# Another written order for the last attention phase of a 1-core kernel, with 34 more constant products on TensorE

## The chip, the cores and the metric

The kernel runs as one program on one core of one Trainium2 chip. The metric is the device time of one execution in microseconds (us). The kernel before took 2472.5 us (median of 3 executions, 2460.71 to 2488.86). All times from the trace are counted from the start of the profiled execution's span.

## The reference, cut to what matters

Two layers act on x, 8 sequences of 512 tokens of 128 features. Layer 0 is an attention with 16 heads of 8 features and a mixture of 16 experts; layer 1 is a gated cumulative mixer and a spiking feed-forward part. The change lies where layer 0's attention ends and its routing begins:

```
logits = S * scale + (G[..., :, None] - G[..., None, :])
P = softmax(where(tri, logits, -1e30));  o = P @ v;  x = x + ga * (o @ Wo)
h = layernorm(x) * (1 + cb) + sb
logits = -sum((h - keys)**2) + h @ rw.T + rb      # 16 experts per token
topv, topi = top_k(logits, 4);  w = softmax(topv)
x = x + gb * sum_k w_k * expert_{topi_k}(h)
```

The kernel sorts the tokens by expert first: for each token it finds the four experts and a row number (a slot) for each of them in a buffer in HBM, sends the token's row there four times, and later runs the experts over that buffer in pages of 128 rows.

## The kernel before, in words

Attention handles one sequence ("batch") at a time, in a **front half** (projections, the recurrence inside chunks of 16 tokens) and a **back half** (scores, softmax, values, output projection). A loop runs the back half of batch b beside the front half of batch b+1. After it there is one more phase, the **last attention phase**: the back half of batch 7 beside the **routing** of batches 0 to 6. The routing of batch 7 comes in the next block, with the experts; then comes layer 1.

In that phase each engine runs one instruction stream, woven of two by a string (`ORDER_END`, one entry per engine: 'pe' TensorE, 've' VectorE, 'act' ScalarE, 'po' GpSimd). A letter takes the next step of a stream: `b` of the back half, `r` of the routing, and `w`, on TensorE alone, one constant product (line 192): the 128x128 identity times itself, in float32, into PSUM bank 3, which nobody reads and for which nothing waits. Each profiled product is two instructions. The steps wait on semaphores for their data. The string decides only what stands ahead of what in an engine's own queue. The strings of before hold 175 `w`.

Back half, the steps in the order of TensorE's queue:
- **Stage A**, the chain of rotations: 7 times four products each of L1109 and L1116 and two of L1123, with copies by ScalarE (L555, L559) and VectorE (L828).
- **Stage B**, the row maxima: 40 jobs in 10 sets of four (m0 to m39). A job opens with L1156; its PSUM bank must have been read by the reduction (L833, VectorE) of the job four before. After the fourth opening come the set's score products (L1166 or L1160), and then the four reductions. Set 0 is m0 to m3.
- **Stage C**: a product of the maxima (L1173), its subtraction from the in-chunk scores on VectorE ("pdx", L853), their transposes ("pdT", L1179), exponentials, and 16 spreading products (rep0 to rep15, L1194), each multiplied on VectorE (L873) and added up half by VectorE (L884), half by GpSimd (oi0 to oi7: L439 and L446). VectorE's product 2i waits for oi(i-2); a rep waits for the product three before it; the stage after waits for all of them.
- **Stage D**, scores, exponentials and values: 14 groups of up to three jobs. S[k] are the group's score products (L1210, L1219, L1222), E[k] the one ScalarE exponential of it (L606), and v the value products (L1234). S[k+1] waits for E[k], since both use the same banks. v4 also waits until VectorE has copied the first block of results away ("raw0", L867).
- **Tail**: sums, transposes, output projection, x (to L939).

Routing of batch b: statistics and normalization (VectorE L1488, L1494, L1500, ScalarE L1442, L1447); transposes xT (L1622); ScalarE L1453, L1457; transposes back (bk, L1629); the **logit step** (four times L1640, L1641 and L1642: 12 products of 16 columns); top-4 on VectorE (L1507 to L1525, "chosen"); the count products (cnt, L1649 and L1650); slots on VectorE up to L1591; transposes and a product for the experts' bias (trn L1657, bia L1663) with VectorE's L1604 and L1610 on x. Then GpSimd sends the batch's rows: 16 indirect DMAs (L1436), 112 in the phase. GpSimd's queue also holds the masked copies "qsm" (L434), which wait for all 40 maxima, and oi0 to oi7.

The phase ends when every engine has done its part; the block of the experts then starts on all of them.

Of the kernel before, what the change touches and what calls it, by code (L numbers as in the profile page):

```python
# [120 lines left out]
def load_small(nc, dram, w, label):  # L121

    loaded = nc.alloc_semaphore(label + "_small")
    with nc.Block() as block:

        @block.sync
        def _(sp):
# [17 lines left out]
ORDER_FIRST = ('fffffffffffffffffffffffwfwffwwwwfwfwffwwwwfwfwffwwwwfwfwffwwwwfwfwffwwwwfwfwfwwfwwfwfwffwwwwfwfwffww'  # L145
           'wwfwfwffwwwwfwfwffwwwffffwwwffffwwfffwwwwwwwfwwwwwwwwwwwwfwwwwwwwwwwwwfwwwwwwwwwf')
ORDER_END = {
    'pe': ('brwwwwbbbbrbbbrrbbrbbbrwbrbbbbbbbwbbbbbbrbrbbbbbrbwwwbbwwwwrbbbbbbrwwbwwbwwbrwbbwwwbwwbwwbwwbbwwwwww'
           'bwwbwwbwwbbwwwrbbwwbwrbrbbbbbbwwbwwbwwbwwbbwbwwbwwbwwwwrbbwbwwbwwrwwwwrbwbbwwwwwwwwwwwwwwbwwwwwrbbww'
           'brrbwwwwwwwwwwwrwwwwwwrwwwwrwwbbwwwwwbbbbbbbbbwwbbwbbwbwrbbbrrbbbbbbwwwwrwbbbbbbbrwwbbbbrwwwbbbbbbbb'  # L150
           'bbwwwwbbbrbbbwrrbbbbbbbbwrbbbbbrbbwwbbbrbbbbwwbbbbbbbwwwwbbbbrbbbbbwrrbbbbbwwwrbbbbrbbbwwbbrrbbbbbbb'
           'bbbwwwbbbbbwwwwwwwwwwbwwwwb'),
    've': ('rrrrbrbbbrrrrrrrrrrrrrrrbbbrrrrrrrbbrrrrbbbrrrrrrrrrrrrrrrbbbbrrrrrbbbbrrrrbbbbrrbbbbbbbbrrbbbbrbbbb'
           'rrrrrrbbrrrrrbbrrrrrrrrrrrbrbbbbbbbbbbrrrrrrrrrrrrrrrbbbbrrrrrrrrrbbbbrbbbbbbbbbrbbbbbbbbbbbrrrrrrrr'
           'rrrrrrrrrrrrrbrrrrbrbrrrrrrrrrrrrrrrrrrrrrrrrrbrrrrrrrrrrrrrrrrrrrrrrrrrbbbbbbbbbbb'),
    'act': ('brrbrrbrrbbbrbbbbrrbbrrrbbbbbbbrbbbrrrrrbrrrrrrrrrrbbbrrrrrrbbrbbrrbrrrbrbrbbrrbrrrbrbrrbbb'),
    'po': ('bbbbbbbrrrrrrrrrrrrrrrrrrrrrrrrrrrrrrrrrrrrrrrrrrbrrrrrrrrrbbrbbbrbbrbrrrrrrrrrrrrrrrrrrrrrrrrrrrrrr'
           'rrrrrrrrrrrrrrrrrrrrrrrrrrrrr'),
}

# [2478 lines left out]
```

## Time and profile before

| | |
|---|---|
| median of 3 executions | 2472.5 us |
| profiled execution: its own time | 2484.16 us |
| profiled execution: span | 2482.4 us |
| mean granted TensorE clock | 0.888 of full |
| TensorE busy over the span | 84% |
| VectorE, ScalarE, GpSimd busy | 65%, 35%, 39% |
| last attention phase | 1461 to 1694 us |

The page gives the busy time of each engine; the last attention phase is about 9% of the span, so stretches of the trace are what is to be read. In a table of stretches each engine has its busy time and, in brackets, its number of instructions; then come the granted clock of TensorE (1.00 is 2.4 GHz, 0.50 is 1.2 GHz), the share of the DMA engines, and GB/s. In a timeline a row has start, duration, engine (PE is TensorE, DVE VectorE, ACT ScalarE, POOL GpSimd), line and operation, what is written and read, and the number of instructions merged into it; a bracket holds the engine's idle time before the row and what ended it. A busy TensorE is one with a product in flight.

### The profile page before, as it was taken

What the parts mean: (1) busy time and instruction counts of PE and PEld (TensorE: products, weight loads), DVE (VectorE), ACT (ScalarE), POOL (GpSimd) and SP (SyncE); (2) the same over time, 40 slices, a digit from 0 to 9 for tenths busy, and PEclk for the clock granted to TensorE, in tenths of its full rate; (3) what the DMA queues carried; (4) which work ended last, traced back from release to release, by engine and by line L of the source; (5) the groups of instructions that cost most, each with busy time, mean ns of one, the idle gap of its engine ahead of it and who ended that gap; (6) DMA issues with size and microseconds to landing.
All of it is one profiled execution on the core that took longest, in us unless ns stands there. A gap on an engine that the chain in (4) does not pass through costs nothing. (4 is left out here: it accounts for less than half of the span.)

```text
span 2482.4 us, 44309 instructions
## 1 busy us (share of the span) xinstructions
PE 2089.1 (84%) x16530; PEld 1388.0 (56%) x16530; DVE 1607.4 (65%) x3446; ACT 861.3 (35%) x1690; POOL 972.2 (39%) x999
## 2 busy tenths in 40 slices
PE   3888988987988988988988989997899982678885
PEld 2563653553663563563564567766899981334443
DVE  5968568568568568568558555733533334789986
ACT  2031331331331331232232222231366643477682
POOL 1514323314323314313313315753555558875221
PEclk7898998998998998898898888877999996799997
DMA  3102002002002002003003001115222221110000
GB/s 101 35 7 81 2 8 79 2 8 80 2 8 79 2 7 80 1 3 85 1 3 85 1 14 35 34 37 192 63 71 71 72 78 40 40 32 26 5 9 13
DMA packets 136618, 98.83 MB, mean 40 GB/s; under 512 B 14754, under 2 KB 127587, under 8 KB 136291
## 3 DMA queue, kind: packets, MB, share of 16 engines
q1 hardware_dynamic: 128226, 79.21, 10.9%
q0 software_dynamic: 8192, 16.79, 2.3%
q8 instruction: 146, 2.39, 0.4%
q14 instruction: 54, 0.43, 0.1%
HBM read 36.25 MB, written 55.57 MB: 37 GB/s over the span
## 5 line engine op out<-in xcount | busy, mean ns | idle before, releaser
L606 ACT ACTIVATE a_prep<-ps 128x1536 f32<-128x1536 f32 (+1 forms) x112 | 155.7, 1391 | 390.2 <-PE ps L1219 240.5
L413 POOL TENSOR_TENSOR a_K<-a_K,a_yU 128x480 f32<-128x480 f32 (+14 forms) x120 | 83.9, 699 | 423.6 <-DVE a_yU L782 423.6
L833 DVE TENSOR_REDUCE a_mpart<-ps 128x4 f32<-128x512 f32 x320 | 198.4, 680 | 62.2 <-PE ps L1160 58.1
L419 POOL TENSOR_TENSOR a_X<-a_X,a_txy 128x480 f32<-128x480 f32 (+14 forms) x240 | 177.8, 755 | 119.1 <-DVE a_txy L787 118.4
L1759 ACT ACTIVATE b_hid<-ps,b_stage 128x128 f32<-128x128 f32 x576 | 164.8, 369 | 138.3 <-PE ps L1863 138.3
L1743 POOL COPY b_stage<-b_w 128x1028 f32 x144 | 150.6, 1046 | 127.3 <-PE ps L1872 127.3
L1038 PE MATMUL ps<-a_txy,cst 128*128 128x480 f32 (+14 forms) x480 | 174.8, 472 | 7.8 <-DVE a_txy L769 7.8
L2003 POOL DMA_INDIRECT c_got<-rows_y,packed x128 | 151.4, 1183 | 38.3 <-issue 35.5
L787 DVE TENSOR_TENSOR a_txy<-a_wf,ps 128x480 f32<-128x480 f32 (+14 forms) x240 | 97.9, 417 | 88.2 <-PE ps L1038 85.7
L1863 PE MATMUL ps<-b_hTp,b_stage 128*128 128x128 f32 x1152 | 153.6, 277 | 0.0
L1872 PE MATMUL ps<-b_stage,b_hid 128*128 128x128 f32 x1152 | 152.3, 275 | 0.3 <-ACT b_hid L1759 0.3
L1436 POOL DMA_INDIRECT rows_h<-a_tS,r_slot x112 | 110.2, 984 | 101.6 <-issue 52.0
L769 DVE TENSOR_TENSOR a_txy<-a_bw,a_X 128x480 f32<-128x480 f32 (+14 forms) x240 | 142.4, 616 | 10.3 <-POOL a_X L419 10.3
L1863 PEld LDWEIGHTS ps<-b_hTp,b_stage 128*128 128x128 f32 x1152 | 141.5, 194 | 0.0
L1872 PEld LDWEIGHTS ps<-b_stage,b_hid 128*128 128x128 f32 x1152 | 140.2, 192 | 0.5 <-ACT b_hid L1759 0.5
L192 PE MATMUL ps<-cst 128*128 128x128 f32 x792 | 125.8, 307 | 14.4 <-PEq L209 14.4
L192 PEld LDWEIGHTS ps<-cst 128*128 128x128 f32 x792 | 112.0, 214 | 32.9 <-issue 28.9
L1156 PE MATMUL ps<-a_aux_g,a_g_hotb 24*128 24x512 bf16 (+1 forms) x320 | 104.2, 429 | 28.0 <-DVE a_mpart L833 26.6
L800 DVE TENSOR_TENSOR a_mats<-ps,cst 128x512 f32<-128x512 f32 x112 | 71.1, 683 | 75.8 <-PE ps L1067 75.8
L1835 DVE COPY b_hTp<-ps 128x128 f32<-128x128 f32 x144 | 41.9, 291 | 119.5 <-PE ps L1863 103.2
L1038 PEld LDWEIGHTS ps<-a_txy,cst 128*128 128x128 f32 x480 | 83.6, 215 | 63.6 <-DVE a_txy L769 34.4
L1032 PE MATMUL ps<-a_tU,cst 128*128 128x480 f32 (+14 forms) x240 | 93.1, 473 | 21.4 <-DVE a_tU L763 20.5
(469 smaller groups left out, 4658.7 us busy)
## 6 DMA issues: line engine op xcount, KB each, us to landing
rows_h<-a_blank SPq DMA_DIRECT2D x66, 512.0 KB, 6.5
b_hrow<-rows_h SPq DMA_DIRECT2D x144, 64.0 KB, 1.8
rows_y<-b_orow SPq DMA_DIRECT2D x144, 64.0 KB, 1.5
b_w<-in_wexp SPq DMA_DIRECT2D x16, 514.0 KB, 11.0
c_got<-rows_y,packed POOLq DMA_INDIRECT x128, 2.6
out<-xs SPq DMA_DIRECT2D x8, 256.0 KB, 2.3
cst<-in_const SPq DMA_DIRECT2D x1, 1865.5 KB, 14.7
rows_h<-a_tS,r_slot POOLq DMA_INDIRECT x112
```

What stands on the lines that cost most here:

```text
L192: nc.tensor.matmul(out, square, square, start=True, stop=True, skip_group_check=True)
L419: nc.gpsimd.tensor_tensor(x, x, yX[:, a, 0:n].rearrange("p (c s) -> p c s", c=NC), ALU.subtract).then_inc(e_uX.sem, 1)
L606: nc.scalar.activation(Pt[:, at:at + width, :], ps[:, 4:4 + width, :], ACT.Exp).then_inc(e_exp.sem, width)
L769: nc.vector.tensor_tensor(by_chunk(tX[:, a, 0:n]), chunks(bw[:, :])[:, :, left], chunks(X2[:, a, :])[:, :, right], ALU.mult).then_inc(e_tX ...
L833: nc.vector.tensor_reduce(mpart[:, i, j, 4 * g:4 * g + 4], ps[:, 4 + n % 4, :].rearrange("p (r j) -> p r j", r=4), AX.X, ALU.max).then_inc ...
L1038: mm(ps[:, 1 + a, 0:n], con("block8"), tX[:, a, 0:n], start=True, stop=True).then_inc(e_pX.sem, 1)
L1436: nc.gpsimd.indirect_dma_start(hrows, bass.IndirectOffsetOnAxis(R.slot[:, n, k:k + 1], 0), R.htok[:, b % 2, t, :], None).then_inc(R.e_sent ...
L1743: nc.gpsimd.tensor_copy(stage[:, p % 3, :], we[:, bass.ds(e, 1), :]).then_inc(e_stage.sem, 1)
L1759: last = nc.scalar.activation(hid[:, p % 2, f, :], ps[:, p % 2, 128 * f:128 * f + 128], ACT.Gelu, bias=stage[:, p % 3, AT_B1 + f:AT_B1 + f ...
L1863: last = mm(ps[:, q % 2, 128 * f:128 * f + 128], stage[:, q % 3, 128 * f:128 * f + 128], hTp[:, q % 2, :], start=True, stop=True, skip_gro ...
L1872: last = mm(ps[:, 4 + r % 2, 0:D], hid[:, r % 2, f, :], stage[:, r % 3, F + D * f:F + D * f + D], start=f == 0, stop=f == NF - 1, skip_gro ...
L2003: nc.gpsimd.indirect_dma_start(got[:, b % 2, k, t, :], None, yrows, bass.IndirectOffsetOnAxis(R.packed[:, n, k:k + 1], 0))\
```

## The change

Only the four strings of `ORDER_END` change. The numbers of `b` and of `r` stay the same on every engine (208 and 44 on TensorE, 98 and 185 on VectorE, 41 and 50 on ScalarE, 16 and 113 on GpSimd); `w` goes from 175 to 209. By stage of TensorE's queue the products are: up to m0 13, now 15; m0 to m39 82, now 87; stage C 33, now 42; from the first score group to cnt6 28, now 46; after that 19 and 19. What moves most:
- TensorE, stage B: logit step 2 goes from ahead of m20 to behind m24; xT2 from ahead of m16 to behind it; cnt2 from ahead of m31 to behind m33; trn2 and bia2 from behind m33 and ahead of m34 to behind m35; six products ahead of m12 become three.
- VectorE, stage B: chosen2 to eq2 (11 routing operations) go from ahead of max28 and max30 to, in the main, behind max31.
- VectorE, stage C: pdx goes behind the rest of routing 3 (L1575 to L1598). TensorE has 14 products instead of 2 ahead of pdT.
- TensorE, stage C: xT4 goes from behind rep12 to behind rep6, bk4 and logit step 4 from behind rep15 to behind rep8; six products then stand ahead of S[0].
- GpSimd: four sends of batch 3, not three, ahead of oi0; three, not one, between oi4 and oi5.
- Stage D: eight products, not four, ahead of cnt4; VectorE does part4, in4 and the statistics of batch 5 (L1604 to L1494) ahead of raw0, and 14 products, not 3, stand between v3 and v4; ScalarE does hT5 and hsq5 (L1453, L1457) ahead of E[4]; logit step 6 goes from the middle of S[10] to behind it; cnt6 from ahead of S[11] to behind it and v31.

```
--- before.py
+++ after.py
@@ -145,16 +145,16 @@
 ORDER_FIRST = ('fffffffffffffffffffffffwfwffwwwwfwfwffwwwwfwfwffwwwwfwfwffwwwwfwfwffwwwwfwfwfwwfwwfwfwffwwwwfwfwffww'
            'wwfwfwffwwwwfwfwffwwwffffwwwffffwwfffwwwwwwwfwwwwwwwwwwwwfwwwwwwwwwwwwfwwwwwwwwwf')
 ORDER_END = {
-    'pe': ('brwwwwbbbbrbbbrrbbrbbbrwbrbbbbbbbwbbbbbbrbrbbbbbrbwwwbbwwwwrbbbbbbrwwbwwbwwbrwbbwwwbwwbwwbwwbbwwwwww'
-           'bwwbwwbwwbbwwwrbbwwbwrbrbbbbbbwwbwwbwwbwwbbwbwwbwwbwwwwrbbwbwwbwwrwwwwrbwbbwwwwwwwwwwwwwwbwwwwwrbbww'
-           'brrbwwwwwwwwwwwrwwwwwwrwwwwrwwbbwwwwwbbbbbbbbbwwbbwbbwbwrbbbrrbbbbbbwwwwrwbbbbbbbrwwbbbbrwwwbbbbbbbb'
-           'bbwwwwbbbrbbbwrrbbbbbbbbwrbbbbbrbbwwbbbrbbbbwwbbbbbbbwwwwbbbbrbbbbbwrrbbbbbwwwrbbbbrbbbwwbbrrbbbbbbb'
-           'bbbwwwbbbbbwwwwwwwwwwbwwwwb'),
-    've': ('rrrrbrbbbrrrrrrrrrrrrrrrbbbrrrrrrrbbrrrrbbbrrrrrrrrrrrrrrrbbbbrrrrrbbbbrrrrbbbbrrbbbbbbbbrrbbbbrbbbb'
-           'rrrrrrbbrrrrrbbrrrrrrrrrrrbrbbbbbbbbbbrrrrrrrrrrrrrrrbbbbrrrrrrrrrbbbbrbbbbbbbbbrbbbbbbbbbbbrrrrrrrr'
-           'rrrrrrrrrrrrrbrrrrbrbrrrrrrrrrrrrrrrrrrrrrrrrrbrrrrrrrrrrrrrrrrrrrrrrrrrbbbbbbbbbbb'),
-    'act': ('brrbrrbrrbbbrbbbbrrbbrrrbbbbbbbrbbbrrrrrbrrrrrrrrrrbbbrrrrrrbbrbbrrbrrrbrbrbbrrbrrrbrbrrbbb'),
-    'po': ('bbbbbbbrrrrrrrrrrrrrrrrrrrrrrrrrrrrrrrrrrrrrrrrrrbrrrrrrrrrbbrbbbrbbrbrrrrrrrrrrrrrrrrrrrrrrrrrrrrrr'
+    'pe': ('brwwwwwbbbbbrbbrrbbbbbbrbbbbrbrbbbbbbbbbbbbbrbwwrrbwwwbbwwwwwrbbbbbrbwwbwwbwwwrbbbwwwbwwbwwbwwbbwwwb'
+           'wwbwwbwwbbwwwwwwwbwwwwwrbbwwbbwbrbbwwbbwbrbbbbwwwbwwbwwbwwbbwwbwwbwrwbwwbbwwwrwwwwrwwwwwwwwwwwwwwbww'
+           'bwwwwrbbrrbwwwwwwwwwwwrwwwwwwrwwwwrwwwwwwwwwwwwwwbbwwwwwbbbbbbbbrbbrrbbbbbwwbbbbwwwwwwbbbbwwwwwwwwrb'
+           'bbrbbbbwwwbbbrbwwwwwwwwwwwwwwbbbbbbbbbbrbbbbbbbrrbbbbbbbwwwrbbbbbwrbbwwbbbrbbbbwwwbbbbbbbwwwwbbbbbwr'
+           'bbbbbrrbbbbbbbbbwrbbwbbbrbbbrrbbbbbbwwwwbbbbbwwwwwwwwwwbwwwwb'),
+    've': ('rrbrrbrbbrrrbbrrbrrrrrrrrrrrrbbrrrrrrbrrbrbrrrrrrrrrrrrrrbbbbrrrrbbbbrrrrbbbbrrrbrbbbbbbbbbbbrrbbbbr'
+           'bbrbbrrrrrrrrrrrrrrrrrrrrrbbrbbbbbbbbrrrrrrrrrrrrrrrbrrrrrrbbbbrrrrbbbbrbbbbbbbbrbrbbbbbbbbbbbrrrrrr'
+           'rrrrrrrrrrrrrrrrrbrbbrrrrrrrrrrrrrrrrrrrrrrrrrbrrrrrrrrrrrrrrrrrrrrrrrrrbbbbbbbbbbb'),
+    'act': ('brrbbrrrbrbbbbrbbbbrrbbbbrrbrbbrbbbrrrrbrrrrrrrrrrrbbrrbrrrbrbrbrrbrrbrbrbrbbrrbrrbrrbbrrbb'),
+    'po': ('bbbbbbbrrrrrrrrrrrrrrrrrrrrrrrrrrrrrrrrrrrrrrrrrrbrrrrrrrrrrbbrbbbrrrbbbrrrrrrrrrrrrrrrrrrrrrrrrrrrr'
            'rrrrrrrrrrrrrrrrrrrrrrrrrrrrr'),
 }
```

## Rows read from the trace of the kernel before

**Rows 1.** Table of stretches, stages B, C and D before cnt6.
```profile
1506.00:1571.00 65.00, 63.88 (x560) 44.96 (x556) 40.41 (x114) 10.85 (x22) 28.08 (x30) 0.84 0.09 30
1571.00:1602.00 31.00, 27.96 (x173) 23.67 (x173) 24.67 (x78) 7.52 (x13) 26.62 (x27) 0.92 0.10 33
1602.00:1668.00 66.00, 65.25 (x665) 44.84 (x666) 23.50 (x114) 20.73 (x25) 39.76 (x41) 0.71 0.13 42
```

**Rows 2.** Timeline, end of the phase.
```profile
1672.79 0.17 DVE L1591 CAST r_slot<-a_gshift 128x16 int32<-128x16 f32 x1
...
1673.74 0.97 POOL L1436 DMA_INDIRECT rows_h<-a_tS,r_slot  x1 [7.96 <-DVE r_slot L1591]
...
1689.81 0.69 DVE L939 TENSOR_TENSOR xs<-xs,a_prep 128x512 f32<-128x512 f32 x1
...
1692.92 0.97 POOL L1436 DMA_INDIRECT rows_h<-a_tS,r_slot  x1 [0.30 <-issue]
```

**Rows 3.** Table of stretches at one level of the clock.
```profile
1532.70:1552.40 19.70, 19.70 (x75) 11.82 (x76) 7.29 (x28) 0.26 (x1) 0.00 (x0) 0.50 0.01 5
1553.20:1573.20 20.00, 18.88 (x139) 14.94 (x139) 15.87 (x48) 2.98 (x6) 11.45 (x12) 1.00 0.10 34
...
1601.00:1614.00 13.00, 13.00 (x140) 10.23 (x140) 5.89 (x33) 3.73 (x4) 9.95 (x11) 0.50 0.15 52
...
1635.00:1648.00 13.00, 13.00 (x92) 7.33 (x94) 5.41 (x30) 3.62 (x4) 1.98 (x3) 0.50 0.02 7
```

**Rows 4.** Timeline, first and last products of logit step 2.
```profile
1529.25 0.39 PE L1640 MATMUL ps<-r_kr,a_txy 128*128 128x16 f32 x2
...
1532.60 0.61 PE L1642 MATMUL ps<-a_bw,a_qf 128*128 128x16 f32 x2
```

**Rows 5.** Timeline, four constant products in a row, twice.
```profile
1548.48 2.08 PE L192 MATMUL ps<-cst 128*128 128x128 f32 x8
...
1578.89 1.06 PE L192 MATMUL ps<-cst 128*128 128x128 f32 x8
```

**Rows 6.** Timeline of VectorE, first reductions of sets 1, 2, 4, 6, 7 and 8.
```profile
1513.40 2.48 DVE L833 TENSOR_REDUCE a_mpart<-ps 128x4 f32<-128x512 f32 x4 [1.67 <-PE ps L1166]
...
1518.66 1.89 DVE L833 TENSOR_REDUCE a_mpart<-ps 128x4 f32<-128x512 f32 x3 [0.35 <-PE ps L1166]
...
1529.23 2.48 DVE L833 TENSOR_REDUCE a_mpart<-ps 128x4 f32<-128x512 f32 x4 [2.15 <-PE ps L1160]
...
1543.71 2.48 DVE L833 TENSOR_REDUCE a_mpart<-ps 128x4 f32<-128x512 f32 x4 [5.01 <-PE ps L1160]
...
1553.16 1.29 DVE L833 TENSOR_REDUCE a_mpart<-ps 128x4 f32<-128x512 f32 x2 [5.99 <-PE ps L1160]
...
1561.91 0.66 DVE L833 TENSOR_REDUCE a_mpart<-ps 128x4 f32<-128x512 f32 x1
```

**Rows 7.** Timeline, first pair product on VectorE, oi0 and oi5 on GpSimd.
```profile
1584.84 1.02 DVE L873 TENSOR_TENSOR a_prep<-ps,a_vown 128x512 f32<-128x512 f32 x2 [0.40 <-PE ps L1194]
...
1588.28 0.62 POOL L439 COPY a_prep<-a_prep 128x512 f32<-128x512 f32 x1
...
1596.10 1.83 POOL L446 TENSOR_TENSOR a_prep<-a_prep 128x352 f32<-128x352 f32 x2 [0.18 <-DVE a_prep L873]
```

**Rows 8.** Timeline, exponentials E[0] to E[4] and the start of logit step 5.
```profile
1604.93 1.45 ACT L606 ACTIVATE a_prep<-ps 128x1536 f32<-128x1536 f32 x1 [1.70 <-PE ps L1219]
...
1611.06 1.45 ACT L606 ACTIVATE a_prep<-ps 128x1536 f32<-128x1536 f32 x1 [4.68 <-PE ps L1219]
...
1617.17 1.45 ACT L606 ACTIVATE a_prep<-ps 128x1536 f32<-128x1536 f32 x1 [3.22 <-PE ps L1219]
...
1624.12 1.45 ACT L606 ACTIVATE a_prep<-ps 128x1536 f32<-128x1536 f32 x1 [5.51 <-PE ps L1222]
...
1627.93 1.45 ACT L606 ACTIVATE a_prep<-ps 128x1536 f32<-128x1536 f32 x1 [2.02 <-PE ps L1219]
...
1630.77 0.40 PE L1640 MATMUL ps<-r_kr,a_txy 128*128 128x16 f32 x2
```

## The prediction

> **What bounds the kernel now.** The edit touches one phase of 233 us in 2482, so I read that phase alone: first tables of stretches, to see which engine is full and at what clock, then the timeline of each stretch, for what a step waits for. In stages B and D TensorE is in flight 63.88 of 65 and 65.25 of 66 us, VectorE far less [rows 1]. But much of it is filling. In stage B 82 of the 175 constant products run; there an opening waits for a reduction, and a product between them costs nothing only while it is shorter than the reduction's 0.6 us. Stage C is looser: TensorE 27.96, GpSimd 26.62 of 31 us [rows 1]. The phase does not end with the back half. Its last VectorE operation starts at 1689.81 and takes 0.69 us; GpSimd sends batch 6's rows until 1692.92 + 0.97 = 1693.9. The 16 sends run from 1673.74, so 1.28 us each, and they begin 0.8 us behind the slots of batch 6 (1672.79 + 0.17) [rows 2]. **The end is the slots of batch 6 plus 21 us**, and whatever shortens only the steps behind cnt6 is worth nothing while GpSimd's tail is the longer by 3.4 us.
>
> **The clock.** It falls around the end of logit steps: step 2 ends at 1532.60 + 0.61 [rows 4], and the clock is at 0.50 from 1532.7 for 19.7 us. In that stretch TensorE is in flight 19.70 of 19.70 us; in the 20 us behind it only 18.88 of 20, at 1.00. Two more long ones are in stage D (13 us each) [rows 3]. At 1.2 GHz four constant products take 2.08 us, at 2.4 GHz 1.06 [rows 5], so 0.52 and 0.27 each: the lower level turns fillings into path. A set of stage B took (1529.23 - 1518.66) / 2 = 5.3 us at the full clock, and 1553.16 - 1543.71 = 9.4 in the low stretch, though VectorE's four reductions take 2.48 in both [rows 6].
> The Trainium skill, "TensorE: Matmul & The Clock Gate", section "Why this matters for your kernels", says that TensorE gets its full clock by being kept busy without a break and loses it in idle gaps. By that rule the 34 products would help. Here the trace differs: the level was low for 19.7 us in which no gap shows [rows 3].
>
> **The change, part by part.** No semaphore and no real operation is added, and the seven logit steps stay. The bare price of the 34 products, if all were path, would be 34 x 0.27 = 9 us or 34 x 0.52 = 18; if all fall into waits, 0. They are costed below where they stand.
>
> *Stage A*: two products more on a full TensorE: +0.5 (0 to +1).
>
> *Stage B, up to m27.* Three products fewer ahead of m12: -0.7. xn2 now stands between max12 and max13 instead of ahead of both: between 0 and +1.1 (four normalizations); I take +1. Logit step 2 leaves set 5 for set 6. Sets 4 to 6 took 1543.71 - 1529.23 = 14.5 us [rows 6], since the step (3.96 us [rows 4]) came first and a whole set then ran at the low clock. Now set 5 runs at the full clock with five products (4.6, a little under 5.3), and the way to set 6 is one reduction, the step, and three openings with their scores: 0.7 + 4.0 + 2.2 = 6.9. Gain 3.0.
>
> *m28 to m31*: nine products in both, cnt2 gone to the next set: -0.9.
>
> *From set 7 to set 8.* It took 1561.91 - 1553.16 = 8.75 us [rows 6]. Now the 11 routing operations, which VectorE did for nothing while TensorE was slow, come behind max31 (about 2.0 us), and trn2 and bia2 come behind the set's scores. Until x is updated and its statistics are taken VectorE doesn't get to max32, and m36 waits for that; the 14 products ahead of m36 fill this wait. At the full clock: reductions 2.5, routing to the slots' end 4.5, wait for bia2 1.4, update and statistics 2.6, so 11.0. At the low clock the set's eight products and scores take 8.7, then come 3 + 4 products (3.6 with trn2, bia2 and ScalarE's copy about 4.3), update and statistics 2.5: 15.5. So +2.3 to +6.7. Which one hangs on the clock behind logit step 2. The stretch is filled in the same way, two products and an opening, and before, with that filling, it stayed low until four products stood in a row behind m30; now the first such place is behind trn2. I take the low end of the clock: +6.7. Stage B: -0.7 + 1.0 - 3.0 - 0.9 + 6.7 = **+3.1**; at the full clock m28 to m31 would also fall from 9.4 to 5.3, and the sum is -0.7 + 1.0 - 3.0 - 4.1 + 2.3 = -4.5.
>
> *Stage C.* pdx comes behind 2.3 us of slot arithmetic, and pdT behind 12 more products (3.2 us, at the low clock 6.2). Before, the first pair product started at 1584.84, but GpSimd came to oi0 only at 1588.28, 2.9 us after the half that it copies was there, because nine sends stood ahead [rows 7]. So GpSimd hides up to 2.9 us of it, and the new order costs what GpSimd's queue costs: one more send ahead of oi0, two more ahead of oi5 (1596.10 before [rows 7]), 3 x 1.28 = +3.8. Who waits: VectorE's pair products 14 and 15, and all of stage D. Against it logit step 4 (3.96) leaves the place between rep15 and S[0] for the time in which VectorE waits for GpSimd: -4.0. Six products ahead of S[0] run beside the last two pair products: +0.2. **0** (-2 to +4; it is +4 if step 4, ahead of rep9, holds up the pair products themselves).
>
> *Stage D.* E[0] to E[1] took 1611.06 - 1604.93 = 6.1 at the low clock [rows 8]. Eight products instead of four: +2.1 low, +1.1 full, but step 4 ended some 5 us earlier, and 14 products in a row are likely to bring the full clock into this pair: -1. E[1] to E[2], 6.1 as well, at the full clock like E[3] to E[4] (3.8 [rows 8]): -2.3. E[2] to E[3] took 6.95. Now raw0 stands behind part4, in4 and statistics, 3.3 us behind bia4, and S[3] behind v4: 1.1 + 3.3 + 0.4 + 1.6 + 0.6 = 7.0; the 14 products (3.7) fill it at the full clock. 0. At the low clock they take 7.3 and are path: +3.6, and v3, v4 and S[3] with them, +4.6. Logit step 5 waited for hT5 and hsq5, which ScalarE did after E[4]: from 1627.93 + 1.45 to 1630.77 = 1.4 us [rows 8]. Both now come ahead: -1.4. **-4.7.**
>
> *Tail.* Logit step 6 behind S[10] shares its time with E[10], but cnt6 now comes behind S[11], v30 and v31, at the low clock that the step leaves. From E[9] the slots of batch 6 come 0.9 us later than before. The back half then ends some 3 us sooner, under GpSimd's sends, for nothing. **+0.9.** If the sends were not the end, this would be -3.
>
> Sum: 0.5 + 3.1 + 0 - 4.7 + 0.9 = **-0.2 us**. The profiled execution's own time was 2484.16 (span 2482.4), 11.7 above the median of the runs; so 2484.0 there, and 2472.5 - 0.2, about **2472** on the scale of the runs. No change.
>
> **Rivals.**
> - *The clock holds* (0.25). The blocks of 14, and 14 ahead of S[1], end the low stretches sooner. Stage B gives -4.5 instead of +3.1, and in stage D one of the two 13 us stretches halves: -6.5. With the rest: -0.2 - 7.6 - 6.5 = -14.3: **2458**. For it: the stretch of 19.7 us ended where four products stood in a row. Against: it follows the logit steps, which stay, and 82 products in stage B didn't prevent it.
> - *The products are path* (0.20). The place is v4 in stage D and pdT in stage C: if the clock is low when the 14 products before them start, they outlast the wait that they fill. +4.6 at v4; 14 x 0.25 = +3.5 at pdT, of which GpSimd still hides 0.6, so +2.9; +3.3 since the gains between E[0] and E[2] don't come; +3 where step 4 holds rep9 up. Sum -0.2 + 4.6 + 2.9 + 3.3 + 3 = +13.6: **2486**. It decides from the point at which a 14-block starts at 0.50. For it: the three low stretches in rows 3 alone make 45.7 us. Against: the long blocks stand far behind logit steps.
> - *No fall without idle* (0.05). If filling alone keeps the level, the three low stretches of rows 3 (45.7 us) run as the full-clock sets do, at 5.3 / 9.4 of their time: -19.9. The way from set 7 to set 8 then costs +2.3 and not +6.7, another -4.4: -0.2 - 19.9 - 4.4 = -24.5, **2448**. This is what the page's rule above would make of the change.
> - *Nothing moves in the order that matters*: excluded, the strings are the queues.
>
> The forecast itself has 0.50. About 1% (24.7 us) is what a measurement of this kernel can tell from no change. The shown runs lie 28 us apart, from 11.8 below the median to 16.4 above, and that is more than any term here. Range: 2450 to 2488, from near the third rival to the second, with that spread. Faster by over 1% is half the third rival, part of the first and chance: 0.09. Slower by over 1% takes the second rival and an unlucky clock: 0.06. Within 1%: 0.85.
>
> **What would show it.** Right: about 230 to 236 us from the phase's start to GpSimd's last send; last send 5 to 8 us behind the back half's end; low stretches behind every logit step, the one of step 2 again near 20 us; max31 to max32 over 7 us; oi0 about 5 us behind the first pair product or less; E[1] to E[2] under 5 us. Wrong: the low stretches together under 40 us, or a block of 14 products that takes over 6 us ahead of v4 or pdT.

## The result, and the profile after

The changed kernel took 2493.11 us in the median of 18 runs (2465.64 to 2509.73), the kernel before 2475.24 in 18 (2460.71 to 2490.28): **a ratio of 1.0074, 95% interval 1.0051 to 1.0096**, so about 18 us slower. The forecast was 2472 in a range of 2450 to 2488; the time lies above it. The profiled execution of the changed kernel took 2488.08 us (span 2486.2, clock 0.886), 5 below its median; that of before lies 9 above its own (2475.24). So the two profiles stand only 3.9 us apart, and the phase, 243.4 us against 232.9, carries 10.5 of loss in them; the code behind the phase, which the edit does not touch, was 6 us shorter in this execution (782.5 us against 788.5).

The table of stretches of the changed kernel, with the columns of [rows 1]: first the phase cut at set 0, set 4, the row maximum "mrow" (L839), E[0] and the last send, then the low stretch:

```profile
1460.40:1510.80 50.40, 44.24 (x339) 40.85 (x340) 22.18 (x103) 18.22 (x42) 22.22 (x22) 0.80 0.11 36
1510.80:1549.90 39.10, 36.38 (x287) 26.90 (x287) 15.59 (x39) 3.04 (x7) 16.73 (x18) 0.56 0.09 31
1549.90:1586.00 36.10, 35.59 (x223) 25.45 (x222) 23.74 (x71) 5.51 (x11) 8.89 (x10) 0.91 0.05 16
1586.00:1619.70 33.70, 32.18 (x247) 27.58 (x248) 24.77 (x85) 7.41 (x13) 28.59 (x29) 0.95 0.10 34
1619.70:1703.80 84.10, 79.73 (x869) 57.81 (x869) 32.09 (x141) 26.45 (x31) 53.16 (x55) 0.84 0.13 44
1512.40:1546.40 34.00, 32.88 (x261) 24.67 (x262) 13.95 (x36) 0.99 (x3) 15.19 (x17) 0.50 0.10 32
```

The kernel before, cut at the same events:

```profile
1461.00:1507.50 46.50, 41.81 (x338) 38.65 (x339) 22.23 (x104) 17.28 (x41) 21.57 (x21) 0.82 0.12 37
1507.50:1529.20 21.70, 21.70 (x280) 15.87 (x278) 15.40 (x37) 5.03 (x11) 15.15 (x17) 1.00 0.15 50
1529.20:1570.90 41.70, 40.58 (x222) 27.79 (x219) 23.92 (x72) 4.32 (x9) 11.63 (x13) 0.75 0.06 19
1570.90:1604.90 34.00, 30.96 (x217) 25.83 (x216) 27.44 (x99) 7.78 (x14) 28.95 (x29) 0.89 0.10 34
1604.90:1693.90 89.00, 83.39 (x845) 59.31 (x845) 30.28 (x124) 26.31 (x30) 53.11 (x54) 0.79 0.12 41
```

One row holds most of the loss. The way from set 0 to set 4 took 39.1 us instead of 21.7, its clock 0.56 instead of 1.00, with nearly the same instructions on TensorE (287 and 280). The other four rows together are -6.9. Behind set 0 a stretch of 34 us at 1.2 GHz begins, the longest low stretch of the phase in either kernel, and TensorE is in flight for 32.88 us of it: the missing 1.12 us are the rest of the wait that the next rows show.

What stands ahead of it shows in the timeline of TensorE of the changed kernel; the bracket is idle time and what ended it:

```profile
1509.37 1.38 PE L1166 MATMUL ps<-a_shared,a_roll_q 32*112 32x64 f32 x56
1513.52 1.01 PE L1657 MATMUL ps<-cst,a_yU 128*16 128x128 f32 x4 [2.78 <-DVE a_gshift L1572]
1514.33 1.06 PE L192 MATMUL ps<-cst 128*128 128x128 f32 x4
```

and of VectorE at the same time:

```profile
1509.71 0.42 DVE L1567 TENSOR_TENSOR a_gshift<-a_gshift,a_bw 128x256 f32<-128x256 f32 x1
1510.77 2.49 DVE L833 TENSOR_REDUCE a_mpart<-ps 128x4 f32<-128x512 f32 x4 [0.64 <-PE ps L1166]
1513.17 0.21 DVE L1572 TENSOR_TENSOR a_gshift<-a_gshift,ps 128x64 f32<-128x64 f32 x1
```

trn1 (L1657) puts its transposes into PSUM where VectorE's L1572 still reads, so it waits for L1572 ("pos+w1", the slot position plus the place within its tile). In the kernel before, L1572 stood ahead of the first reduction max0, and L1657 started with no wait:

```profile
1507.38 0.60 PE L1657 MATMUL ps<-cst,a_yU 128*16 128x128 f32 x4
```
```profile
1506.75 0.21 DVE L1572 TENSOR_TENSOR a_gshift<-a_gshift,ps 128x64 f32<-128x64 f32 x1
1507.47 2.48 DVE L833 TENSOR_REDUCE a_mpart<-ps 128x4 f32<-128x512 f32 x4 [0.51 <-PE ps L1166]
```

The new string of VectorE has L1572 behind max3, so four reductions (2.49 us) come first. TensorE's own queue keeps trn1 right behind the scores of set 0. So TensorE stands idle for 2.78 us, from 1510.7 to 1513.5, and the clock is at 0.50 from 1512.4 on: it falls within the wait.

Set by set, VectorE's reductions of the changed kernel (those of before are [rows 6]): sets 0, 1, 2, 4, 6, 7, 8, and then mrow:

```profile
1510.77 2.49 DVE L833 TENSOR_REDUCE a_mpart<-ps 128x4 f32<-128x512 f32 x4 [0.64 <-PE ps L1166]
1523.30 2.48 DVE L833 TENSOR_REDUCE a_mpart<-ps 128x4 f32<-128x512 f32 x4 [8.56 <-PE ps L1166]
1532.57 2.49 DVE L833 TENSOR_REDUCE a_mpart<-ps 128x4 f32<-128x512 f32 x4 [5.32 <-PE ps L1166]
...
1549.86 2.48 DVE L833 TENSOR_REDUCE a_mpart<-ps 128x4 f32<-128x512 f32 x4 [4.52 <-PE ps L1160]
...
1561.97 2.48 DVE L833 TENSOR_REDUCE a_mpart<-ps 128x4 f32<-128x512 f32 x4 [1.33 <-PE ps L1160]
1567.69 1.29 DVE L833 TENSOR_REDUCE a_mpart<-ps 128x4 f32<-128x512 f32 x2 [2.50 <-PE ps L1160]
...
1578.85 1.25 DVE L833 TENSOR_REDUCE a_mpart<-ps 128x4 f32<-128x512 f32 x2
...
1586.07 0.70 DVE L839 TENSOR_REDUCE a_mrow<-a_mpart 128x64 f32<-128x320 f32 x1
```

A set took 9.27 us (1532.57 - 1523.30), as the low sets of before did, against 5.3 at the full clock. From set 0 to set 4 the loss is 39.1 - 21.7 = 17.4 us. The wait of 2.78 us is a part of it; the sets at the low clock are the other, some 14.6.

### The profile page after: what moved, and what is told of

Read it like the earlier page. It is cut to its first block and busy times, and to the rows that moved or that the text cites. A ratio compares the mean times of both kernels' runs of the same rounds, so it can differ in the third digit from the quotient of the medians.

```text
span 2486.2 us, 44437 instructions
## 1 busy us (share of the span) xinstructions
PE 2094.8 (84%) x16590; PEld 1399.4 (56%) x16598; DVE 1607.8 (65%) x3446; ACT 859.9 (35%) x1690; POOL 965.9 (39%) x999
## 5 line engine op out<-in xcount | busy, mean ns | idle before, releaser
L192 PE MATMUL ps<-cst 128*128 128x128 f32 x860 | 136.0, 310 | 13.6 <-PEq L209 13.6
L192 PEld LDWEIGHTS ps<-cst 128*128 128x128 f32 x860 | 122.1, 217 | 31.9 <-issue 28.6
L1032 PE MATMUL ps<-a_tU,cst 128*128 128x480 f32 (+14 forms) x240 | 92.7, 471 | 21.8 <-DVE a_tU L763 20.9
## 6 DMA issues: line engine op xcount, KB each, us to landing
cst<-in_const SPq DMA_DIRECT2D x1, 1865.5 KB, 14.6
```

Of the source, the lines that this page charges most:

```text
L192: nc.tensor.matmul(out, square, square, start=True, stop=True, skip_group_check=True)
```

## Theories

- **W, the wait.** pos+w1 behind max3 leaves TensorE without work for 2.78 us; the clock falls; in sets 1 to 4 TensorE is the path at the low level. Moving one letter back undoes it.
- **P, the products.** The 34 further products are path, wherever they stand, that is, the phase gets longer by the time that they take.
- **S, the sets.** The products between the openings (25 of them between trn1 and m15) are path at the low clock, and it depends on them how long it stays there. S does not exclude W.

The expectations below name further rivals where they need them (R, F, K and L) and say what each means.

All experiments edit `ORDER_END` alone. Ratios are to the kernel before on the same chip. Places in the phase are given in us from its start; in the changed kernel set 0 is at 50.4, set 4 at 89.5, mrow at 125.7, E[0] at 159.3.

## One letter of VectorE's string

The edit of the changed kernel (pos+w1 ahead of max0, not behind max3):

```
-    've': ('rrbrrbrbbrrrbbrrbrrrrrrrrrrrrbbrrrrrrbrrbrbrrrrrrrrrrrrrrbbbbrrrrbbbbrrrrbbbbrrrbrbbbbbbbbbbbrrbbbbr'
+    've': ('rrbrrbrbbrrrbbrrbrrrrrrrrrrrrbbrrrrrrbrrbrbrrrrrrrrrrrrrrrbbbbrrrbbbbrrrrbbbbrrrbrbbbbbbbbbbbrrbbbbr'
```

> The changed kernel with pos+w1 (L1572) ahead of max0 on VectorE; 209 products. Theory W: at least 10 us faster than the changed kernel beside it, ratio 0.995 to 1.002, set 0 to set 4 about 22 us. Theory P: within 3 us of the changed kernel.

Beside it ran the changed kernel itself as a control, unedited:

> The changed kernel, unaltered, as the control of the other three on their chip. In the runs before it the last attention phase took some 80 us longer than in the first profiles, with TensorE's constant products issued one by one (idle until issue), so the comparison of the moved letters has to be made beside the changed kernel itself. Where the phase runs as in the first profiles: ratio 1.005 to 1.010. Theory W (trn1 waits for L1572, the clock falls at set 1) expects a low stretch of 20 us or more from set 0 or 1 on; theory P (34 products more) expects it too.

The control took 2495.52 us (ratio 1.006, 1.003 to 1.009), with the wait (2.77 us) and the low stretch (34.1 us) again. With the letter moved: 2479.88 us, ratio 1.0004 (0.997 to 1.0038), and 15.6 us less than the control (difference of the medians; the two ratios differ by 0.0056, which is 14 us). Its timeline of TensorE behind set 0, and its table of stretches from set 0 to 4 and on to mrow:

```profile
1515.05 1.38 PE L1166 MATMUL ps<-a_shared,a_roll_q 32*112 32x64 f32 x56
1516.36 0.60 PE L1657 MATMUL ps<-cst,a_yU 128*16 128x128 f32 x4
```
```profile
1516.40:1538.20 21.80, 21.80 (x290) 16.30 (x286) 15.39 (x37) 3.89 (x10) 12.73 (x14) 1.00 0.13 43
1538.20:1575.90 37.70, 37.21 (x227) 25.63 (x223) 23.81 (x71) 5.60 (x12) 14.49 (x16) 0.86 0.08 28
```

No bracket on L1657, clock 1.00, 21.8 us as before the change. All 34 further products are in this kernel and by its ratio it is as fast as the one without them: P falls as the account of the loss.

The reverse edit in the kernel before (pos+w1 from ahead of max0 to behind max3):

```
-    've': ('rrrrbrbbbrrrrrrrrrrrrrrrbbbrrrrrrrbbrrrrbbbrrrrrrrrrrrrrrrbbbbrrrrrbbbbrrrrbbbbrrbbbbbbbbrrbbbbrbbbb'
+    've': ('rrrrbrbbbrrrrrrrrrrrrrrrbbbrrrrrrrbbrrrrbbbrrrrrrrrrrrrrrbbbbrrrrrrbbbbrrrrbbbbrrbbbbbbbbrrbbbbrbbbb'
```

> The kernel before with pos+w1 (L1572) behind max3 on VectorE; 175 products. Theory W: ratio 1.004 to 1.009 with a low stretch from set 1 on; its first run gave 1.004 (1.0002 to 1.0078). Theory P: 1.000 to 1.002.

2494.36 us, 1.0033 (1.0005 to 1.0061): slower, from one letter. It is 11.4 us by the medians and 8 by the ratio, which lies a little under the 1.004 expected. The timeline's row, and the table's from set 0 to 4:

```profile
1496.09 1.01 PE L1657 MATMUL ps<-cst,a_yU 128*16 128x128 f32 x4 [2.78 <-DVE a_gshift L1572]
```
```profile
1493.30:1527.90 34.60, 31.82 (x283) 23.27 (x281) 15.70 (x39) 4.75 (x10) 17.46 (x19) 0.65 0.11 37
```

The same wait, a low stretch of 23.9 us behind it, and 34.6 us instead of 21.7.

## The wait taken away, or filled, on TensorE's side

The letter of VectorE moves its order as well. So trn1 was moved instead, behind opening m5, with pos+w1 left behind max3:

```
-    'pe': (...'bbbbbrbwwbwwbwwwrbbb'...
+    'pe': (...'bbbbbbwwbwwbrwwwrbbb'...
```

> The changed kernel with one letter of TensorE's string moved: the transpose trn1 (L1657) stands behind opening m5 instead of right behind the scores of set 0, so VectorE's pos+w1, which stays behind max3, is done before TensorE comes to it. Theory W (TensorE's 2.8 us without work there drops the clock, and the low level makes sets 1 to 4 long): no wait before L1657, no low stretch of 34 us from there, mrow near 109 to 115 us from the phase's start instead of 125.7, phase 230 to 237 us, a ratio near 1.000. Rival S (VectorE's order of pos+w1 and the products between the openings are what makes the sets long, the wait is only beside it): the low stretch and mrow at 125 stay, ratio 1.006.

And the wait was left where it is, with ten more products (2.7 us at the full clock) directly ahead of trn1:

```
-    'pe': (...'bbbbbrbwwbww'...
+    'pe': (...'bbbbbwwwwwwwwwwrbwwbww'...
```

> The changed kernel with ten more constant products (10 x 0.27 = 2.7 us at the full clock) directly ahead of trn1 (L1657), so that TensorE works through the 2.78 us in which it waited for VectorE's pos+w1; nothing else is moved, and trn1 itself comes at the same time. Theory W in the form 'the idle time drops the clock': the level stays at 1.00 behind trn1, mrow near 109 to 115 us instead of 125.7, phase 230 to 237 us, ratio near 1.000. Rival (the fall follows logit step 1, whatever TensorE does in the wait, as it did behind step 2 of the kernel before, with no gap): the clock falls within a few us all the same, sets 1 to 4 stay near 9.3 us each, mrow 125 to 128, ratio 1.006 or over.

trn1 later: 2475.64 us, ratio 1.0009 (0.9977 to 1.004); the wait filled: 2487.25, ratio 1.0051 (1.0013 to 1.0089). Timeline at L1657 and table of the stretch from set 0 to 4, first of the kernel with trn1 later:

```profile
1509.80 0.60 PE L1657 MATMUL ps<-cst,a_yU 128*16 128x128 f32 x4 [0.66 <-DVE a_gshift L1572]
```
```profile
1507.00:1529.80 22.80, 22.01 (x290) 16.31 (x286) 15.58 (x38) 3.30 (x8) 12.80 (x14) 1.00 0.12 41
```

and of the one with the wait filled:

```profile
1515.00 2.50 PE L192 MATMUL ps<-cst 128*128 128x128 f32 x20
1517.85 0.60 PE L1657 MATMUL ps<-cst,a_yU 128*16 128x128 f32 x4 [0.35 <-DVE a_gshift L1572]
```
```profile
1515.10:1539.70 24.60, 24.25 (x306) 18.57 (x306) 15.57 (x38) 3.11 (x8) 11.31 (x13) 1.00 0.10 33
```

In the second, trn1 comes as late as in the changed kernel (4.15 us behind the start of the scores of set 0: 1517.85 - 1513.70 here, 1513.52 - 1509.37 there); only the idle time is gone. The clock stays at 1.00 and 24.6 us do instead of 39.1, 2.9 more than before the change: the delay itself. So at this place and in these traces the clock falls with the idle time, and neither with the late trn1 nor with VectorE's order alone. The times do not confirm this for the filled kernel. It should have come near 1.000, and its interval leaves 1.000 out; its median is 11.7 us over before, of which the delay explains 2.9. Its 12 runs go from 2466.38 to 2503.16, and only one of them was profiled, with a phase of 232.8 us. Whether the clock fell in the others is not shown. In times the case for the wait rests on n1, n2 and y5, and each of these took the wait away or put it in by moving a step.

The Trainium skill, "TensorE: Matmul & The Clock Gate", section "Why this matters for your kernels", asks to leave no long idle gaps between bursts of matmuls, or the clock drops. At this place the traces agree: 2.78 us of idle time and a fall in all six profiles of the five kernels that had it (the changed kernel was profiled twice), 0.35 and 0.66 us and no fall in these two. Its other half, that being busy brings the clock back, they do not bear out: 32.88 of 34 us in flight at 0.50.

The length of a gap alone does not decide. In the changed kernel's own profile, in layer 1, TensorE stood idle just as long, and the clock stayed at 1.00:

```profile
2322.73 1.98 PE L2455 MATMUL ps<-c_hT,s_fc 128*128 128x512 f32 x4 [2.77 <-ACT c_hT L2175]
```
```profile
2316.00:2345.00 29.00, 21.57 (x79) 11.28 (x77) 28.69 (x47) 26.89 (x48) 11.26 (x5) 1.00 0.03 9
```

Likewise the splice n6 below waits 2.65 us in stage C (L1622, at 1588.26) at a clock of 1.00 from 1585.6 to 1594.0. Why the gap in set 0 is followed by a fall each time and these two are not is not shown.

## Which part carries the loss

Two kernels were spliced from the two sets of strings. The cut is at mrow, on each engine at its own step there. Of each edit VectorE's line is shown, cut short:

```
# n7_first_half: changed up to mrow, before's from there
-    've': ... 'bbrbbrrrrrrrrrrrrrrrrrrrrrbbrbbbbbbbbrrrr ...
+    've': ... 'bbrbbrrrrrrrrrrrrrrrrrrrrrbbrbbbbbbbbbrrr ...
# n6_end_only: before up to mrow, changed from there
-    've': ... 'rrrrrrbbrrrrrbbrrrrrrrrrrrbrbbbbbbbbbbrrr ...
+    've': ... 'rrrrrrbbrrrrrbbrrrrrrrrrrrbrbbbbbbbbbrrrr ...
```

> Stages A and B in the changed order, from mrow on in the order before; 7 of the 34 added products are in. Theory W: all of the loss and none of the end's gain: ratio 1.006 to 1.011, as slow as the changed kernel or slower. Theory P: 1.001 to 1.003, since 27 of the products are out.

> Stages A and B in the order before, from mrow on in the changed order; 27 of the 34 added products are in. Theory W, after the kernel with the halves the other way round (phase 252.2 us, the changed one 243.3, that before 232.9 in their profiles): the end of the phase gains some 5 to 9 us, ratio 0.996 to 0.999. Theory P (added products are path): 1.003 to 1.006.

The first half alone: 2500.8 us, 1.0075 (1.0049 to 1.0102), the whole loss, with the wait (2.78) and the low stretch (34.1). The second half alone: 2481.25, 0.9983 (0.9949 to 1.0017): nothing that can be measured. So stages A and B carry it, as the sum of terms below says too.

The profile of the second half alone shows one more thing. Up to mrow it has the strings of before, but its low stretch behind logit step 2 is 3.4 us long, not 20.5, and set 4 to mrow took 34.4 us, not 41.7. So the same order gives stage B some 7 us more or less from one profile to the next.

## What the products between the openings do

The changed kernel without the 25 products between trn1 and m15 (the wait stays), and with 14 products in a row ahead of m8 where three stood:

```
# x8_sets_bare
-    'pe': (...'bbbbbrbwwbwwbwwwrbbbwwwbwwbwwbwwbbwwwb' 'wwbwwbwwbbwww'...
+    'pe': (...'bbbbbrbbbrbbbbbbbbbbbbbwww'...
# x9_block_of_14
-    'pe': (...'rbbbwwwbwwbww'...
+    'pe': (...'rbbbwwwwwwwwwwwwwwbwwbww'...
```

> The changed kernel without the 25 constant products between trn1 and m15 (sets 1 to 3), all else as changed; the wait ahead of trn1 stays. Theory S (once low, the clock stays low in these sets, and there the products between two openings are path, 0.43 us each): sets 1 to 3 take about 6 us each and not 9.3, 10 us in all, ratio 1.001 to 1.004. Rival F (the products are harmless filling, the low clock alone makes the sets long): the sets stay at 9 us, ratio 1.005 to 1.009. Rival K (the products shorten the low stretch): the low stretch grows beyond 34 us and the ratio is over 1.009.

> The changed kernel with 14 products in a row ahead of m8, where it has 3 (220 products in all). It asks what ends the low stretch. Theory S: a row of products at 1.2 GHz ends it, so the stretch that begins at set 1 is over before set 3; the block costs about 5 us and sets 2 to 4 win about 3 us each: ratio 1.002 to 1.007, low stretch 17 us or less. Rival L (the level returns after a certain time or only at a logit step, whatever TensorE does): the stretch stays 34 us and the block is on the path: 1.007 to 1.010.

The first took 2487.03 us, 1.0039 (1.0007 to 1.0071); the second 2500.29, 1.01 (1.006 to 1.014). For each, set 0 to set 4 and then a low stretch (of the second, its later one):

```profile
1507.10:1533.50 26.40, 22.02 (x237) 14.84 (x237) 15.58 (x39) 3.04 (x7) 12.41 (x14) 0.61 0.10 34
1509.00:1529.00 20.00, 17.52 (x205) 11.96 (x206) 12.95 (x34) 0.99 (x3) 7.65 (x8) 0.50 0.09 28
```
```profile
1521.40:1554.10 32.70, 29.99 (x309) 23.34 (x309) 15.57 (x39) 3.04 (x7) 14.19 (x16) 0.79 0.09 31
1561.00:1587.00 26.00, 26.00 (x97) 16.58 (x98) 10.52 (x41) 0.26 (x1) 2.58 (x3) 0.50 0.02 5
```

Without the products the wait (2.78) still drops the clock, but sets cost 5.3 us at the low level instead of 9.3, and the way to set 4 is 26.4 us instead of 39.1. **The half of S on the price holds** in the profiles: at 1.2 GHz those products are path. The runs agree in direction (1.0039 against 1.006 of the control), but the two intervals overlap. The low stretch was 20.5 us without them and 34.1 with them, so they did not bring the clock back. The block of 14 did go with an earlier end: 13.7 us instead of 34.1. It bought nothing: the time, 1.01, is what the expectation gave the rival L and not S. Set 0 to set 4 took 32.7 us with it, and a stretch of 27.3 us at the low clock came later, from 1560.5; in the 26.0 us of it that the table shows TensorE had no idle time at all. One profile each; what ends a low stretch is not settled by them.

## The best of both

Before's strings up to set 0 (stage A), the changed ones from there, with pos+w1 ahead of max0:

```
 # x10_best_mix
-    've': (... 'bbbrrrrrrrrrrrrrrrbbbbrrrrrbbbbrrrrbbbbrrbbbbbbbb'...
+    've': (... 'bbbrrrrrrrrrrrrrrrbbbbrrrbbbbrrrrbbbbrrrbrbbbbbbb'...
```

> Stage A in the order before (which reached set 0 3 to 4 us earlier), then the changed order with pos+w1 (L1572) ahead of max0, so stage B's later part and the end as changed. Theory W: all three gains without the loss, ratio 0.994 to 0.999. Theory P: 1.003 to 1.006 for its 32 added products. If stage A's order was only a shift of the clock's falls: 0.998 to 1.002.

2476.03 us, ratio 0.9995 (0.9967 to 1.0023). Its profile has the shortest phase of all (223.0 us, set 0 at 47.1, mrow at 105.0, E[0] at 138.7), but by the runs it is no faster than the kernel before, and the 0.994 to 0.999 expected of theory W did not come. No version beats the kernel before measurably.

## Four runs on a chip that issues this phase slowly

The first four kernels ran on another chip. There the kernel before took 2574.93 us (35 runs), 92 to 100 more than on the others.

> The changed kernel with one letter moved on VectorE: pos+w1 (L1572) stands ahead of max0 again, as before the change; TensorE's string is the changed one, with its 209 products. Theory W (a new wait: trn1 (L1657) is queued on TensorE behind the openings' score products and waits for L1572, which the change put behind four reductions; TensorE idles 2.8 us, the clock falls at set 1 and stays low for 34 us, in which the products between openings are path): the idle time ahead of trn1 is gone, set 0 to set 4 takes about 22 us instead of 39, ratio to the kernel before 0.995 to 1.001. Theory P (the 34 added products are path by themselves): the time stays at 1.005 to 1.009. Theory R (routing arithmetic moved behind max31 and the later rows): 1.005 to 1.009 too.

> The kernel before with the one letter moved the other way: pos+w1 (L1572) behind max3 on VectorE, all else as before, 175 products. Theory W: the wait of 2 to 3 us ahead of trn1 appears, a low stretch of 20 to 34 us begins at set 1, ratio 1.004 to 1.009. Theory P: only the wait itself, 1.000 to 1.002. Theory R: 1.000 to 1.002.

> The changed kernel with one letter moved on TensorE: trn1 stands behind m5 and not ahead of m4, so that four products and two openings lie between S of set 0 and trn1; VectorE as changed. Theory W: TensorE has work while VectorE comes to L1572, no long idle time ahead of trn1; if the fall at set 1 comes from that idle time, the ratio is 0.996 to 1.002, close to the kernel with L1572 ahead. Theories P and R: 1.005 to 1.009.

> Stages A and B in the order before, everything from the product of the maxima (mrow on VectorE, mback on TensorE) on in the changed order; so 27 of the 34 added products are in. Theory W: the changed end gains the 4 to 5 us that the two profiles show from mrow to the last send (1693.9 - 1570.9 = 123.0 before, 1703.8 - 1586.1 = 117.7 after), ratio 0.996 to 1.000. Theory P: 27 products more, 1.003 to 1.006. Theory R: the end is neutral, 0.999 to 1.001.

e1 (the letter of n1): 2567.28, 0.9994 (0.9957 to 1.003). e2 (that of n2): 2585.48, 1.004 (1.0002 to 1.0078). e5 (trn1 behind m5): 2576.52, 1.0016 (0.9982 to 1.005). e6 (the second half alone): 2577.32, 1.0013 (0.9975 to 1.005). Only the interval of e2 leaves out 1.000, as that of n2 does. The phase took 311 to 324 us and its queues were late by themselves, so the times say nothing more. The profile of e2 has the wait of trn1 again (2.78 us), and 34.1 us at 1.2 GHz from 1.7 us behind it on. Waits of TensorE in the phase of e1, in us in total, times, and the longest:

```profile
PE ps L1219 <- issue: 11.2, 11, 1.9
PE ps L192 <- issue: 8.8, 11, 1.8
PE ps L1629 <- ACT a_txy L1453: 8.4, 3, 4.5
PE ps L1156 <- DVE a_mpart L833: 6.9, 4, 6.0
```

"issue" is time in which nothing that the profile shows was waited for. In the same code on an ordinary chip (n1) TensorE has no wait put down to "issue" in the phase, and L1629 waits 0.8 us in two. So the four were run again on other chips, as n1, n2, y5 and n6.

## Why the prediction was wrong, point by point

**The step that failed** is "Stage B, up to m27". It costed three products, xn2 and logit step 2, and took sets 0 to 4 as they were. It did not follow pos+w1, a step of routing 1, past max0 to max3, though the diff of the strings shows it, and so did not ask who waits for it. It asked of xn2 what waits behind a moved step, and not here. Term by term, from the profiled phases (before, then after):

- Stage A: forecast +0.5; 46.5 to 50.4, **+3.9**. TensorE waits 0.40 us for L1453 ahead of bk1 (L1629), and the low stretch behind the second logit step is 6.8 us instead of 3.4. The stretch is not the cause: n1 and y5 have 3.4 us there and still reach set 0 at 49.8 and 50.4. x10, with the order of before in stage A, reaches it at 47.1. The cost is real in the profiles, too small for the runs, and what makes it up is open.
- Set 0 to set 4: forecast -0.7 + 1.0; 21.7 to 39.1, **+17.4**. The failed step.
- Set 4 to set 6: forecast -3.0; 14.5 to 12.1 (1561.97 - 1549.86), -2.4. The size is right, but n6, with the order of before, took 11.0 here. So the clock of one profile makes as much as the order, and the gain is not shown.
- Set 6 to 7: forecast -0.9 at the low clock or -4.1 at the full; 9.45 to 5.72, -3.7. Set 7 to 8: forecast 15.5 at the low clock, 11.0 at the full; 11.16. Both sizes for the full clock were right, but the clock chosen was the other one: the stretch behind logit step 2 was 6.8 us (from 1556.7), not near 20. The condition on which +6.7 was chosen failed here, to the good side. As n6 shows (3.4 us), that stretch can be short with the old order too.
- Set 8 to mrow: not forecast; 8.98 to 7.22, -1.8, the full clock again.
- Stage C (mrow to E[0]): forecast 0; 34.0 to 33.7. oi0 comes 2.1 us behind the first pair product (1604.82 - 1602.70, rows below), where it came 3.4 behind it before, so GpSimd's one more send does not hold the stage up. In n1 the stage took 39.8 us, with a low stretch of 13.7 us from 1598.8 on; in the other profiles with the new order it took 33.6 to 36.3.
- Stage D and tail: forecast -4.7 + 0.9 = -3.8; 89.0 to 84.1, **-4.9**. Right, and the end is again batch 6's slots plus 21 us (1682.73 to 1702.78 + 0.97). More profiles bear it out: on the chips with the usual time this part took 83 to 87 us in the nine with the new order, and 89 to 92 in the three with the old one.

Set 0 to mrow is +17.4 - 2.4 - 3.7 + 2.4 - 1.8 = +11.9, and the phase +3.9 + 11.9 - 0.3 - 4.9 = +10.6 (10.5 by its ends) against a forecast of -0.2. Of the +17.4 of the failed step the wait is 2.8 and the low clock some 14.6. The rows that answer to [rows 2], [rows 5], [rows 7] and [rows 8], from timelines of the changed kernel:

```profile
1576.21 3.39 PE L192 MATMUL ps<-cst 128*128 128x128 f32 x28
...
1602.70 1.02 DVE L873 TENSOR_TENSOR a_prep<-ps,a_vown 128x512 f32<-128x512 f32 x2 [2.56 <-PE ps L1194]
...
1604.82 0.62 POOL L439 COPY a_prep<-a_prep 128x512 f32<-128x512 f32 x1
...
1623.83 1.45 ACT L606 ACTIVATE a_prep<-ps 128x1536 f32<-128x1536 f32 x1 [2.51 <-PE ps L1219]
...
1628.84 1.45 ACT L606 ACTIVATE a_prep<-ps 128x1536 f32<-128x1536 f32 x1 [3.10 <-issue]
...
1682.73 0.17 DVE L1591 CAST r_slot<-a_gshift 128x16 int32<-128x16 f32 x1
...
1700.43 0.69 DVE L939 TENSOR_TENSOR xs<-xs,a_prep 128x512 f32<-128x512 f32 x1
...
1702.78 0.97 POOL L1436 DMA_INDIRECT rows_h<-a_tS,r_slot  x1 [0.30 <-issue]
```

Of the signs set down before, those of an error did not show: the blocks of 14 took 3.39 us, never over 6, and the low stretches of the phase came to 92 us together, not under 40. Right were max31 to max32 (8.5 us, over 7) and oi0; E[1] to E[2] took 5.01, at the edge. Wrong were the length of the phase (243.4, not 230 to 236), the stretch behind step 2, and the last send, 2.6 us behind the back half's end instead of 5 to 8.

**The rivals.** "The products are path" named a place (v4, pdT) that stayed at the full clock here, and the times of n1 and n6, which have the products there, show no loss. "The clock holds" came true in part: from set 4 to the end of the phase the mean clock was 0.88 against 0.80, and it was outweighed. "No fall without idle" is refuted: behind logit step 2 the clock was at 0.50 from 1556.7 for 6.8 us in which TensorE was in flight throughout, and no gap since the one in set 0 was over 0.24 us. The true case was in none: a new wait of TensorE in set 0 that costs 2.8 us by itself and five times as much through the clock. The range had no room for a wait that was not seen; that is where it was too narrow.

Of the loss in the runs (about 18 us), the one letter gives back 15.6 on one chip (14 by the ratios). The remaining difference is within what these runs can tell.

## What to carry to other kernels

When two engines' queues are reordered by hand, go through every step that changed its neighbour on one engine and look up who waits for it on the others: here one VectorE operation of 0.21 us, moved behind four reductions, made TensorE wait 2.78 us. Price an idle gap of TensorE not by its length alone but also by what the following code would cost at the lower clock: here 14.6 us on top of 2.8. Look in the trace whether the clock does fall there, since it did not behind every gap of this length. Fill work that hides in waits at the full clock is path at the low one, so a densely padded stretch has the most to lose from such a gap (39.1 us to set 4 with the padding, 26.4 without). Remove the wait first (one letter, or the waiting step a little later), and pad after.

## What the runs showed of the hardware

- A gap of 2.78 us in set 0 was followed by a fall to 1.2 GHz each time: 34.1 us long in the changed kernel, the control, the splice n7 and e2, 23.9 in n2, 20.5 in x8 and 13.7 in x9. In the changed kernel TensorE was in flight for 97% of it. The time at the low clock bears no relation to the length of the gap.
- A gap of 2.77 us in layer 1 and one of 2.65 us in stage C of n6 were followed by no fall for 22 and 5.7 us. So these traces give no length of gap that decides.
- The low stretch was shorter with less filler (20.5 us) and with a block of 14 (13.7 us), in one profile each; filler of two products between openings did not raise the clock.
- On another chip the kernels took 87 to 101 us longer. In their profiles the phase was 76 to 96 us longer, with TensorE's instructions issued late. The effect sought is smaller than that, so a comparison needs a chip on which the kernel before takes its usual time.
